# Graph attention, 8192 nodes: x loads issued by GpSimd, a column sum ended one row tile later, the last row tile ended on VectorE

## The reference

```
h      = relu(layernorm(x))                       # x: 8192 x 256
g      = inlayer2 @ W.T + b                       # 8192 x 128
logits = (g @ w1 + b1)[:, None] + (g @ w2 + b2)[None, :]
coefs  = softmax(leaky_relu(logits, 0.01) + (-1e9 where adj == 0))
out    = x + coefs @ h                            # adj: 8192 x 8192 int32
```

## Time and profile before

| | us |
|---|---|
| median of 3 runs (1448.3 to 1449.22) | 1448.55 |
| profiled execution, its own time | 1447.21 |
| its span, from the first to the last instruction | 1445.4 |
| TensorE matmul busy in the span | 1408.1 (97%) |
| TensorE's share of the chain that ended last | 94% |
| VectorE busy | 1279.7 (89%) |
| ScalarE busy | 612.4 (42%) |
| GpSimd busy | 267.6 (19%) |

### The profile page before, as it was taken

How to read it: one execution, slowest core, us unless ns; L and a number is a source line. 1 busy time by engine, 2 the same in 40 slices (tenths; PEclk the granted TensorE clock), 3 DMA queues, 4 the chain that set the end, 5 groups by cost and what they waited for, 6 DMA issues and landing times.

```text
span 1445.4 us, 33386 instructions
## 1 busy us (share of the span) xinstructions
PE 1408.1 (97%) x12623; PEld 1246.3 (86%) x12623; DVE 1279.7 (89%) x1313; ACT 612.4 (42%) x714; POOL 267.6 (19%) x269
## 2 busy tenths in 40 slices
PE   8489999999999999999999999999999999999998
PEld 7377888888888888888888888888888888888887
DVE  5899999989899898989989898998989989898994
ACT  2895344344444343444434344343434434344430
POOL 0582111101111110111111011111101111110111
PEclk9789999999999999999999999999999999999999
DMA  9978999999999999999999999999999999999940
GB/s 301 310 181 181 234 230 230 231 232 220 208 211 215 209 211 209 215 209 210 215 209 210 207 216 211 209 215 209 210 207 217 209 211 215 207 212 207 215 103 8
DMA packets 110168, 302.43 MB, mean 209 GB/s; under 512 B 11716, under 2 KB 44612, under 8 KB 110148
## 3 DMA queue, kind: packets, MB, share of 16 engines
q1 hardware_dynamic: 100144, 289.58, 89.4%
q10 hardware_dynamic: 10004, 12.59, 2.9%
HBM read 293.73 MB, written 8.39 MB: 209 GB/s over the span
## 4 chain that ended last, share of the span: by engine, by line
PE 94%; ACT 2%; DVE 2%; DMA 1%; issue 1%; ACTq 0%; POOL 0%; SPq 0%; POOLq 0%; DVEq 0%
PE acc L1024 61%; PE acc L1026 30%; PE rp L979 2%; DMA adj_sb<-in_adj_dram 1%; DVE wgt L824 1%; ACT h_f L570 1%; DVE wT L834 0%; ACT H L576 0%; PE rp L993 0%; ACT o_room L584 0%; DMA w<-in_L_gnn_w_dram 0%; PE small L966 0%; ACT rp L554 0%; DVE b_word L810 0%; ACT mask L554 0%
## 5 line engine op out<-in xcount | busy, mean ns | idle before, releaser
L1024 PE MATMUL acc<-H,wT 128*128 128x257 f16 x8192 | 1356.2, 273 | 9.7 <-DVE wT L834 6.9
L1026 PE MATMUL acc<-H,wT 128*128 128x257 f16 x4096 | 1120.0, 273 | 0.0
L1024 PEld LDWEIGHTS acc<-H,wT 128*128 128x128 bf16 x8192 | 802.1, 98 | 113.0 <-DVE wT L834 6.9
L554 ACT ACTIVATE mask<-adj_sb 128x1024 bf16<-128x1024 int32 x504 | 519.2, 1053 | 542.8 <-DVE wgt L824 428.8
L834 DVE STREAM_TRANSPOSE wT<-wgt 128x1024 f32<-128x1024 f32 x512 | 634.0, 1239 | 129.2 <-PE acc L1026 129.1
L824 DVE SCALAR_TENSOR_TENSOR wgt<-b_word,c_word,mask 128x1024 f32<-128x1024 f32 x504 | 626.9, 1256 | 0.0
L1026 PEld LDWEIGHTS acc<-H,wT 128*128 128x128 f16 x4096 | 401.5, 98 | 50.5
L474 POOL TENSOR_TENSOR x_res<-o_room,x_res 128x256 f32<-128x256 f32 x64 | 66.5, 1039 | 1115.2 <-ACT o_room L561 1069.5
L561 ACT ACTIVATE o_room<-acc,r_den 128x256 f32<-128x256 f32 x64 | 30.2, 471 | 251.0 <-DVE r_den L853 251.0
L479 POOL TENSOR_TENSOR o_room<-o_room,x_res 128x256 f32<-128x256 f32 x64 | 82.3, 1287 | 5.3
L476 POOL TENSOR_SCALAR o_room<-h_mean,no_nb 128x256 f32<-128x256 f32 x64 | 60.8, 950 | 0.0
(11 more groups left out here) (91 smaller groups left out, 173.2 us busy)
## 6 DMA issues: line engine op xcount, KB each, us to landing
adj_sb<-in_adj_dram SPq DMA_DIRECT2D x504, 512.0 KB, 8.6
x_res<-in_x_dram SPq DMA_DIRECT2D x64, 128.0 KB, 4.0
out_dram<-o_room SPq DMA_DIRECT2D x64, 128.0 KB, 4.2
H<-in_x_dram ACTq DMA_DIRECT2D x16, 256.0 KB, 12.2
H<-in_x_dram SPq DMA_DIRECT2D x16, 256.0 KB, 12.7
adj_sb<-in_adj_dram ACTq DMA_DIRECT2D x8, 512.0 KB, 13.1
wgt<-in_L_gnn_inlayer_dram ACTq DMA_DIRECT2D x8, 256.0 KB, 9.0
wgt<-in_L_gnn_inlayer_dram SPq DMA_DIRECT2D x8, 256.0 KB, 9.6
```

Of the source, the lines that this page charges most:

```text
L554: nc.scalar.activation(place, adj_sb[:, c, g * CQ:(g + 1) * CQ], ACT.Relu, scale=M_SCALE).then_inc(m_ready, 1)
L1024: pe.matmul(acc[:, par, 0:DV], w_hi[:, slot, t, :], H[:, j, part, 0:DV], start=(j == 0 and part == 0), stop=False)
L1026: mm = pe.matmul(acc[:, par, 0:DV], w_lo[:, slot, t, :], H[:, j, 0, 0:DV], start=False, stop=(j == ROWS - 1))
```

## The change

Four edits in one:

1. The far halves of x strips 1 to 7 (14 DMAs of 256 KB) are issued by GpSimd, at the head of its program, each pair behind a wait for an earlier load: strip 1 behind inlayer2 strip 5, strips 2 and 3 behind inlayer2 strip 6, strip 4 behind inlayer2 strip 7, and strips 5, 6, 7 behind the far halves of strips 1, 2, 3. They have semaphores of their own, and each reader of an x strip waits for both. ScalarE's program no longer has them; its far half of adj, row tile 0, chunk 0, now follows `squares(0)` with no x load between.
2. `h_sum` moves on VectorE from ahead of the last two weights of row tile 2, chunk 0, to behind the first weights of its chunk 1; the matmul that spreads it moves from ahead of row tile 2 to behind its second strip; `h_mean` from the third turn of row tile 2 to the sixth.
3. Row tile 63's output is made by VectorE in two instructions from the accumulator, in place of one on ScalarE and three on GpSimd.
4. Its store is split: partitions 0 to 63 on SyncE, 64 to 127 on ScalarE.

```
@@ gpsimd @@
+            for k, begun_after in ((1, in2_loaded[5]), (2, in2_loaded[6]), (4, in2_loaded[7])):
+                pool.wait_ge(begun_after, 64)
+                load_far_x(pool, k)
+                if k == 2:
+                    load_far_x(pool, 3)
+            for k in range(5, NS):
+                pool.wait_ge(xs_far_loaded[k - 4], 32)
+                load_far_x(pool, k)
...
             def finish(I, par, half):
+                if is_row(I, ROWS - 1):
+                    return
@@ scalar @@
             sums(0)
-            load_x(act, 1, 2, (2, 3))
             f_to_sbuf(0)
-            load_x(act, 2, 3, (2, 3))
             squares(0)
-            load_x(act, 3, 4, (2, 3))
             first_adj(act, 0, (2, 3))
-            load_x(act, 4, 5, (2, 3))
             sums(1)
             f_to_sbuf(1)
-            load_x(act, 5, 6, (2, 3))
             squares(1)
-            load_x(act, 6, 7, (2, 3))
-            load_x(act, 7, 8, (2, 3))
...
-            for i in range(2):
-                scale_rows(ROWS - 2 + i, i, ROWS // 2 - 1)
+            scale_rows(ROWS - 2, 0, ROWS // 2 - 1)
+            act.wait_ge(last_ready, 1)
+            act.dma_start(out_rows[ROWS - 1][P // 2:P], o_sb[P // 2:P, 1, :]).then_inc(last_stored, 16)
@@ vector @@
             finish_2(0, 0, 0)
-            dve.wait_ge(h_sum_done, 1)
-            nc.vector.tensor_scalar(h_sum[:, :], hs_ps, 1.0 / (H_SCALE * N), None, ALU.mult).then_inc(h_sum_ready, 1)
             weights(2, 2, 0)
...
             for step in (finish_0, finish_1, finish_2):
                 step(ROWS - 1, 1, ROWS // 2 - 1)
+            nc.vector.scalar_tensor_tensor(out=x_res[:, 1, :], in0=acc[:, 1, 0:D], scalar=r_den[:, 1:2],
+                                           in1=x_res[:, 1, :], op0=ALU.mult, op1=ALU.add).then_inc(last_sum, 1)
+            dve.wait_ge(last_sum, 1)
+            nc.vector.scalar_tensor_tensor(out=o_sb[:, 1, :], in0=h_mean[:, :], scalar=no_nb[:, 1:2],
+                                           in1=x_res[:, 1, :], op0=ALU.mult, op1=ALU.add).then_inc(last_ready, 1)
@@ tensor @@
             products(1, 1, 7)
-            pe.wait_ge(h_sum_ready, 1)
-            pe.matmul(hm_ps, ones[:, :], h_sum[:, :], start=True, stop=True).then_inc(h_mean_ps_ready, 1)
             pe.wait_ge(scaled, 1)
```

More of the change, by code:

```diff
@@ L196, in graph_attention @@
         xs_loaded = [sem(f"xs_loaded{i}") for i in range(NS)]
+        xs_far_loaded = [sem(f"xs_far_loaded{i}") for i in range(NS)]
         zeroed = sem("zeroed")
@@ L258, in graph_attention @@
         o_ready = sem("o_ready")
+        last_sum = sem("last_sum")
+        last_ready = sem("last_ready")
+        last_stored = sem("last_stored")
         o_stored = [sem(f"o_stored{i}") for i in range(2)]
@@ L347, in load_x, with load_far_x, wait_x @@
                 load_strip(eng, x_stage(k), x_q, k, xs_loaded[k], quadrants)
+        def load_far_x(eng, k):
+            load_strip(eng, x_stage(k), x_q, k, xs_far_loaded[k], (2, 3))
+        def wait_x(eng, k):
+            if k == 0:
+                eng.wait_ge(xs_loaded[k], 64)
+            else:
+                eng.wait_ge(xs_loaded[k], 32)
+                eng.wait_ge(xs_far_loaded[k], 32)
         def first_loads(eng, quadrants):
@@ L385, in _ @@
             row_tiles(sp, body, ahead=1)
-            for i in range(2):
-                sp.wait_ge(o_ready, ROWS - 1 + i)
-                sp.dma_start(out_rows[ROWS - 2 + i], o_sb[:, i, :]).then_inc(o_stored[i], 16)
+            sp.wait_ge(o_ready, ROWS - 1)
+            sp.dma_start(out_rows[ROWS - 2], o_sb[:, 0, :]).then_inc(o_stored[0], 16)
+            sp.wait_ge(last_ready, 1)
+            sp.dma_start(out_rows[ROWS - 1][0:P // 2], o_sb[0:P // 2, 1, :]).then_inc(o_stored[1], 16)
             for i in range(2):
                 sp.wait_ge(o_stored[i], 16 * ROWS // 2)
+            sp.wait_ge(last_stored, 16)
         @block.gpsimd
@@ L587, in sums @@
             def sums(k):
-                act.wait_ge(xs_loaded[k], 64)
+                wait_x(act, k)
                 for t in range(TS):
@@ L763, in raw_stats @@
                     if j == first or j % TS == 0:
-                        dve.wait_ge(xs_loaded[j // TS], 64)
+                        wait_x(dve, j // TS)
                     nc.vector.bn_stats(out=pair_stats[:, j // 2, :],
@@ L951, in body @@
                             finish_previous(finish_0)
-                    if is_row(I, 2) and u == 2:
+                    if is_row(I, 2) and u == 0:
+                        dve.wait_ge(h_sum_done, 1)
+                        nc.vector.tensor_scalar(h_sum[:, :], hs_ps, 1.0 / (H_SCALE * N), None,
+                                                ALU.mult).then_inc(h_sum_ready, 1)
+                    if is_row(I, 2) and u == 5:
                         dve.wait_ge(h_mean_ps_ready, 1)
@@ L958, in _ @@
                 step(ROWS - 1, 1, ROWS // 2 - 1)
+            dve.wait_ge(fin_step, 3 * ROWS)
+            dve.wait_ge(x_loaded[1], 16 * ROWS // 2)
+            dve.wait_ge(o_stored[1], 16 * (ROWS // 2 - 1))
+            dve.wait_ge(h_mean_done, 1)
+            nc.vector.scalar_tensor_tensor(out=x_res[:, 1, :], in0=acc[:, 1, 0:D], scalar=r_den[:, 1:2],
[3 more added lines that the diff above has]
+                                           in1=x_res[:, 1, :], op0=ALU.mult, op1=ALU.add).then_inc(last_ready, 1)
         @block.tensor
@@ L1080, in body @@
                     products(I, par, k)
+                    if is_row(I, 2) and k == 1:
+                        pe.wait_ge(h_sum_ready, 1)
+                        pe.matmul(hm_ps, ones[:, :], h_sum[:, :], start=True,
+                                  stop=True).then_inc(h_mean_ps_ready, 1)
             row_tiles(pe, body, ahead=1)
```

## The result

The change made the kernel slower: 1464.04 us median (1461.56 to 1466.5) against 1448.87 (1448.3 to 1449.22), a ratio of 1.0105 with a 95% interval of 1.0093 to 1.0117. The forecast was 1445.2 and the range ended at 1447.9. The profiled execution took 1463.45 us, its span 1461.6, against 1447.21 and 1445.4: 16.2 us more.

A forecast was written before the change was run, and what follows sets the result against it. TensorE was taken as the bound from 133 to 1439 us, leaving only its start and what follows to change. First stage +0.4, row tile 2 -1.6, end -2.1 sum to -3.3: 1448.55 to 1445.2 us, range 1442.6 to 1447.9.

The forecast's parts named there:

- The first stage: Before TensorE's long run: issues saved on ScalarE are given back by x strips 1 and 2 coming later; +0.4 us.
- The third queue takes more than its share: Rival, first stage: x strip 1 comes 6.5 us late, VectorE's packing moves +3.2, total 1448.0 us; chance 0.20.
- Loads in time: Rival, first stage: far halves come early, adj doesn't delay near ones, the whole 1.6 us is gained, 1443.2; chance 0.22.
- GpSimd comes late: Rival, first stage: slow load issues on GpSimd delay its scaling of D_big; at 2.0 us each, 1452.1 us; chance 0.07.
- a wait for VectorE: One way to GpSimd's lateness: VectorE's two-port mode blocks its descriptor writing, up to 1.25 us per load, 1448.8; chance 0.03.
- Row tile 2: Start of row tile 2: VectorE no longer waits for the column sum, so TensorE's waits nearly vanish; -1.6 us.
- The later mean: Row tiles 3 and 4: later h_mean delays adj load and mask about 5 us, just covered before TensorE; taken as 0.
- the fourth rival: The later mean starves TensorE at row tile 3 or 4 by 1 to 2 us, 1446.2 to 1447.2; chance 0.08.
- The end: After the last reciprocal: two VectorE instructions replace 3.07 us on ScalarE and GpSimd, -2.1 us; split store 0, with 0.3 either way.

The follow-up runs named there:

- e1: The change with its first edit alone undone, ScalarE again issuing the far halves of x strips 1 to 7: 1450.91 us, ratio 1.0015 to the kernel before.
- e3: The kernel before with the second edit alone (later column sum, mean copied behind the sixth turn of row tile 2): 1452.19 us, ratio 1.0025.
- e4: The kernel before with the last row tile's output on VectorE and its store in one DMA on SyncE, not split: 1447.2 us, ratio 0.9989.
- g3: The kernel before with the second edit, but the mean copied behind the fourth turn of row tile 2, not the sixth: 1446.76 us, ratio 0.9985.
- f1: The kernel before with the first edit alone, GpSimd's loads each cut into odd and even partitions, 28 issues in place of 14: 1461.71 us, ratio 1.0091.
- g2: The kernel before, no loads on GpSimd, SyncE's near halves of x strips 1 to 7 read in 4 KB pieces (rows permuted): 1463.2 us, ratio 1.0099.
- g1: The kernel before with the first edit alone, SyncE's near halves of x strips 1 to 7 read in 4 KB pieces (rows permuted): 1452.89 us, ratio 1.0028.
- e2: The kernel before with the first edit alone, GpSimd issuing the far halves of x strips 1 to 7: 1462.4 us, ratio 1.0094.
- f3: The kernel before with GpSimd issuing all four quadrants of x strips 1 to 7 and SyncE none: 1464.06 us, ratio 1.0104.

## Why the prediction was wrong

**The first stage** is the step that failed: "both come 3.0 to 4.5 us later, if queues share the engines evenly, which no row proves". Strip 1 came 11.8 us later and strip 2 17.5, and the term that I had at +0.4 measured +13.9 (some 1.3 of it because the trace of before has its packing that much earlier than e1, e3, e4 and g3). The queues share the engines evenly in packets, not in bytes. I had added up which bytes would stand beside the near half, and asked how large a packet is of no queue. The trace of before held the answer in part. Its DMA view from 41 to 44 us, when ScalarE's adj pieces met SyncE's x pieces:

```profile
q10 hardware_dynamic: 201, 0.56, 64.6%
q1 hardware_dynamic: 201, 0.39, 43.6%
```

The packets are the same in number there too, the bytes are not. What it could not show was that GpSimd's DMAs of 1 KB rows would go in packets of 4 KB; the page of the change shows it in one line (1120 packets, 3.67 MB). The Trainium skill ("DMA: Bandwidth & Descriptors", Queues, rings and completion order) has the rule that I should have weighed: each DMA engine goes round the queues and changes only at the end of a packet. The trace agrees: 608 packets against 597. The Trainium skill ("DMA: Bandwidth & Descriptors", SWDGE vs HWDGE vs iDMA) also says of the descriptors that GpSimd builds that a packet is preferably of up to 4096 B. The 4.1 KB of f1 agree.

The rival *The third queue takes more than its share* (0.20) had the right sign of being wrong (`sums(1)` at 43 or later), but not the cause, since g2 starves a queue with two; and it was priced at 6.5 us of lateness and 1448.0, a size that nothing bounded. A queue that gets a fifth of the bytes in place of half can be late by several times that, and this tail should have been in the range. *Loads in time* and *GpSimd comes late* are refuted (the latter by the 0.58 us of an issue, and by f1, with 28 issues at no cost). Nor did a wait for VectorE lengthen an issue: the longest in the change and in f1 are 0.82 and 0.76 us.

**Row tile 2** was right in mechanism, and in size as far as the runs can tell: -1.6 forecast, -2.3 measured in g3 (interval -0.9 to -3.5).

**The later mean** failed too, at "Just covered. I take 0". The load's lateness of 5 us was right (145.05 in e3, 139.90 in the earlier trace rows), and TensorE had no wait for VectorE there, so the count for masks, weights and turns held too. What I left out is that the scaling of the row tile before stands behind those masks on ScalarE, and that TensorE waits for it as well. ScalarE's timeline before the change:

```profile
165.62 0.46 ACT L561 ACTIVATE o_room<-acc,r_den 128x256 f32<-128x256 f32 x1
```

TensorE wants it 14 strips after 132.58, near 169.5, so it was early by some 3.4 us (my estimate from the earlier trace rows). Later by 5.5 (171.08 in e3), with TensorE 1.8 earlier, it is late by the 3.9 measured. The wait is 3.3 to 4.1 us in three traces; with what came behind it, it cost 5.8 us between e3 and g3, where the fourth rival had 1 to 2 at 0.08.

**The end**: the term -2.1 measured -1.4. VectorE's part was right (2.0 saved); the split store, taken as 0 with 0.3 either way, cost 0.5 to 0.6.

So the sum +0.4 - 1.6 + 0 - 2.1 = -3.3 should have read +13.9 - 1.6 + 5.3 - 1.4 = +16.2 for the profiled executions; the medians are 15.2 apart.

## What to carry to other kernels

Before a load moves to another queue, compare the packets that each queue moves (the page's third part: MB over packets), not only bytes and issue times: a queue of 1 KB packets beside one of 4 KB got about a fifth of the bytes here, and the loads that suffered were those that were not touched. If only the issue time is in the way, move the issue behind the urgent instruction on its own engine first; here that took 2.6 us off, more than the exposed wait in one profile said. And where a result is made later, follow every instruction that stands behind it in order on each engine, and put the time beside each of the consumer's waits, not only the one that comes to mind.

## What was not expected of the hardware

- DMAs with the same 1 KB rows go in packets of 1 KB from SyncE and ScalarE, and of about 4 KB from GpSimd, even when the DMA takes every second row only, so that no two of its rows touch in memory (f1: 896 packets with data for 3.67 MB).
- The DMA engines moved 329 GB/s with two queues of mostly 1 KB packets, 290 with two of 4 KB (g1), and 261 to 273 with one of each (the change, e2, f1, g2), busy for nine tenths or more of nearly every slice each time. Why the mixture is slowest stays open.
- GpSimd's issues cost it 0.53 to 0.59 us each in the median and at most 0.82, in the change, e2, f1, f3 and g1, and never held up its work here.
- A wait of TensorE of 3.3 and 4.1 us was followed by some 3.4 us at the lower clock level in two traces (e1, the change), and by none in a third, where the wait was 3.9 us (e3). What decides it stays open.
